# Turning the block mask on the matmul engine instead of by a DMA transpose

## The chip, the cores and the metric

The kernel runs on one core of one Trainium2 chip. The metric is the device time of one execution in microseconds. The engines are TensorE (PE, the matmul engine, with its weight loads shown apart as PEld), VectorE (DVE), ScalarE (ACT), GpSimd (POOL) and the sync engine (SP), which issues DMAs.

## The reference

One decoder block on x of 64 sequences of 128 tokens with 256 features, all fp32: gated causal cross attention with 16 heads against a context, then a gated feed-forward network of 1024 hidden units in 16 blocks, of which each token uses the four that a router picks.

```python
x = x + tanh(g_xattn) * attention(layernorm(x), ctx, ctx)      # 16 heads of 16, causal
xf = layernorm(x)
prob = softmax(xf @ w_router + b_router)
_, idx = top_k(prob, 4)
mask = (idx[:, :, None] == arange(16)).any(axis=1)             # token x block, 0 or 1
h = relu(einsum('nd,ebd->neb', xf, w1b) + b1b)                 # 16 blocks of 64
y = einsum('neb,ebd,ne->nd', h, w2b, mask) + b2
x = x + tanh(g_ffn) * y
```

## The kernel before

A tile is one sequence: 128 tokens on the 128 partitions. The kernel is one software pipeline over iterations i from -4 to 71. In iteration i each engine works, in an order written out by hand, on several tiles at once: scores of tile i + 1, exponentials of tile i, attention output of tile i - 1, the second layernorm of tile i - 2. The feed-forward part works on pairs of tiles (256 tokens): pair p has its hidden pieces 0 and 1 in iteration 2p + 5 and pieces 2 and 3 in iteration 2p + 6, and the output products of tile b stand in iteration b + 7. The engines are tied together by semaphores alone.

The matmul engine's order in an iteration is: scores (L273, L283), transposes of q (L240) and of k (L251), one hidden piece (L380 to L382; each product is split into three of high and low parts), half of an output tile (L401 to L403), in every second iteration the router's logits (L352), attention output (L313), shifted scores (L300), the transpose of the normalised x (L339), in every second iteration the turned logits (L360), the second hidden piece, the second output half, and the transposes of the attention output (L328). L313, L273 and L352 use narrow tiles of the array, the other large groups its full width.

Routing. In iteration 2p + 4 VectorE finds the four largest logits of each token of pair p (L611 to L623) and leaves them marked. ScalarE's choice (L485) turns the marks into a bf16 mask `used`, tokens on partitions, 128 columns for each of the pair's two tiles. The hidden units lie on partitions, so the mask must be turned. In iteration 2p + 5 the sync engine does so with one DMA transpose per pair into `used_all` (L793, in `used_spread`). It waits for the choice and, from pair 2 on, until the masks of two pairs before are done with. VectorE multiplies the hidden pieces by `used_all` in `hidden_masked` (L603), which waits for the transpose at a pair's first piece. The same sync queue then carries the maxima rows (`max_row`, L774: qT to qT, needed by the shifted scores), the loads and the stores.

A hidden piece is written to a bank that the engine may only reuse when L603 has read it (L374). ScalarE makes the relu parts h_high and hid (L475, L476) from the masked piece, and GpSimd makes h_low (L705). Bank M1 (number 7) is shared in turn by the transposes of q, the router's logits, the turned logits and the transposes of the attention output; M0 (number 6) by those of k, the attention output and the transposes of x. After iteration 64 hidden pieces and output tiles alternate between two banks each, since the scores' banks are free by then.

Of the kernel before, what the change touches and what calls it, by code (L numbers as in the profile page):

```python
# [33 lines left out]
def build(nc, A_x, A_ctx, A_g_xattn, A_g_ffn, A_w_router, A_b_router, A_w1T, A_b1, A_w2T, A_b2, out):  # L34
# [24 lines left out]
    with ctx:  # L59
# [92 lines left out]
        q_copied, k_copied, exp_done = sem("q_copied"), sem("k_copied"), sem("exp_done")  # L152
        att_copied, x_copied, xT_high_made = sem("att_copied"), sem("x_copied"), sem("xT_high_made")
        hid_clipped, w_high_made = sem("hid_clipped"), sem("w_high_made")
        route_copied, used_made, tanh_done = (sem(n) for n in ("route_copied", "used_made", "tanh_done"))

        numbers_set, filler_set = sem("numbers_set"), sem("filler_set")
        q_zeroed, q_levels_set, place_zeroed, mask_made = (sem(n) for n in (
# [70 lines left out]
        def _(pe):  # L229
# [87 lines left out]

            def out_transposed(b):
                s = b % 2
                pr = router_pair(b + 1)  # L320
                pe.wait_ge(att_copied, b + 1)
                pe.wait_ge(q_copied, min(b + 4, N + MAX_LAG))
                if pr is not None:
                    pe.wait_ge(clipped_made, PAIR * (pr + 1))
                if b + 3 >= N + MAX_LAG:
                    pe.wait_ge(att_made, b)
                for g in range(U):
                    turned = pe.transpose(banks[M1][:, g * P:(g + 1) * P], oT[:, s, g * S:(g + 1) * S], ident[:])  # L328
                turned.then_inc(att_turned, 1)
# [26 lines left out]
            def logits_transposed(p):  # L356
                if p == 0:
                    pe.wait_ge(adding_made, 1)
                pe.wait_ge(route_copied, p + 1)
                pe.matmul(out=banks[M1][:, 0:PAIR * PAD], lhsT=logitT[:], rhs=adding[:].rearrange("p t e -> p (t e)"),  # L360
                          start=True, stop=True).then_inc(route_turned, 1)

            def hidden(p, m):
                ps = p % 2
# [43 lines left out]
            for i in ITERATIONS:  # L408
                pr, pu = router_pair(i), used_pair(i)
                p, m = hidden_pair(i)  # L410
                out_b = out_tile(i)
                if i + 1 == 0:
                    pe.wait_ge(mask_made, 2 * U)
                if 0 <= i + 1 < N:
                    scores(i + 1)
                if 0 <= i + 2 < N + MAX_LAG:
                    q_transposed(i + 2)
                if 0 <= i + 2 < N:
                    k_transposed(i + 2)
                if p is not None:  # L420
                    hidden(p, m)
                if out_b is not None:
                    ffn_out(out_b, 0)
                if pr is not None:
                    router_logits(pr, i)
                if 0 <= i - 1 < N:
                    attention_out(i - 1)
                if 0 <= i < N:
                    shifted_scores(i)
                if 0 <= i - 2 < N:  # L430
                    x_transposed(i - 2)
                if pr is not None:
                    logits_transposed(pr)
                if p is not None:
                    hidden(p, m + 1)
                if out_b is not None:
                    ffn_out(out_b, 1)
                if 0 <= i - 1 < N:
                    out_transposed(i - 1)

        @block.scalar
        def _(act):
            def q_evacuated(b):
                act.wait_ge(q_turned, b + 1)
                act.copy(qT[:, b % TS, :], banks[M1][:]).then_inc(q_copied, 1)

            def k_evacuated(b):
                act.wait_ge(k_turned, b + 1)
                act.copy(kT[:, b % TS, :], banks[M0][:]).then_inc(k_copied, 1)

            def exponentials(b):
                act.wait_ge(rescored, b + 1)
                for half in range(2):
                    act.activation(weights[:, b % 2, half * 2 * HB:(half + 1) * 2 * HB, :].rearrange("p h q -> p (h q)"),  # L454
                                   score_banks[:, 2 * half:2 * half + 2].rearrange("p u n -> p (u n)"),
                                   ACT.Exp, scale=SCALE).then_inc(exp_done, 1)

            def out_copied(b):
                act.wait_ge(attended, b + 1)
                act.copy(oT[:, b % 2, :], banks[M0][:]).then_inc(att_copied, 1)  # L460

            def x_copies(b):
                p, t = divmod(b, PAIR)
                turned = banks[M0][:, 0:D].rearrange("p (c s) -> p c s", s=S)
                act.wait_ge(x_turned, b + 1)
                act.copy(xT[:, :, t, :], turned).then_inc(x_copied, 1)
                if t == 0 and p >= 2:
                    act.wait_ge(hidden_made, PIECES * (p - 1))
                act.copy(xT_high[:, p % 2, :, t, :], turned).then_inc(xT_high_made, 1)

            def hidden_parts(p, m):
                n = PIECES * p + m
                chunks = slice(PC * m, PC * (m + 1))
                act.wait_ge(hid_made, HC * p + PC * (m + 1))
                act.activation(h_high[:, p % 2, chunks], hid[:, n % 4], ACT.Relu)  # L475
                act.activation(hid[:, n % 4], hid[:, n % 4], ACT.Relu).then_inc(hid_clipped, 1)  # L476

            def choice(p):

                act.wait_ge(marked_made, PAIR * (p + 1))  # L480
                if p == 0:
                    act.wait_ge(numbers_set, 2)
                else:
                    act.wait_ge(used_turned, 16 * p)
                act.activation(used[:], marked[:].unsqueeze(3).to_broadcast([P, PAIR, BLOCKS, UNITS]), ACT.Relu,  # L485
                               scale=2.0 / TAKEN, bias=minus_one[:]).then_inc(used_made, 1)

            def weights_high(i):
                for n in pieces_of(i):
                    w, stage, high, _low = w_piece(n)  # L490
                    act.wait_ge(w_landed[w], 16 * W_LOADS[w])
                    act.copy(high, stage).then_inc(w_high_made, 1)

            act.wait_ge(x_landed[1], 16)
            act.dma_start(w1_stage[:].rearrange("p k e c r -> p k (e c r)"),
                          A_w1T.rearrange("(k p) n -> p k n", p=P)).then_inc(w_landed[0], 16)
            for i in ITERATIONS:
                pr, pu = router_pair(i), used_pair(i)
                p, m = hidden_pair(i)
                if 0 <= i + 2 < N + MAX_LAG:  # L500
                    q_evacuated(i + 2)
                if 0 <= i + 2 < N:
                    k_evacuated(i + 2)
                if pr is not None:
                    act.wait_ge(routed, pr + 1)
                    if pr == 0:
                        act.wait_ge(br_landed, 16 * PAIR)
                    act.activation(logitT[:], banks[M1][:, 0:S], ACT.Identity, bias=br_rows[:]).then_inc(route_copied, 1)
                if 0 <= i - 1 < N:
                    out_copied(i - 1)  # L510
                if 0 <= i < N:
                    exponentials(i)
                if p is not None:
                    hidden_parts(p, m)
                if pr is not None:
                    choice(pr)
                if 0 <= i - 2 < N:
                    x_copies(i - 2)
                if p is not None:
                    hidden_parts(p, m + 1)  # L520
                weights_high(i)
                if i == 0:
                    act.wait_ge(gates_landed, 32)
                    act.activation(tanh_g[:], gates[:], ACT.Tanh).then_inc(tanh_done, 1)

        @block.vector
        def _(dve):
# [63 lines left out]
            def hidden_masked(p, m):  # L591
# [3 lines left out]
                    dve.wait_ge(b1_landed, 16 * HC)  # L595
                    dve.wait_ge(w_low_made, 8)
                if m == 0:
                    dve.wait_ge(used_turned, 16 * (p + 1))
                if n >= 4:
                    dve.wait_ge(h_low_made, n - 3)  # L600
                for j in range(PC):
# [155 lines left out]
        def _(sync):  # L757
# [28 lines left out]
                sync.dma_start(br_rows[rows], A_b_router.rearrange("(e o) -> e o", o=1)).then_inc(br_landed, 16)  # L786
            for c in range(KC):
                sync.dma_start(w_router[:, c, 0:BLOCKS], A_w_router[c * P:(c + 1) * P, :]).then_inc(small_landed, 16)
            def used_spread(p):
                if p >= 2:  # L790
                    sync.wait_ge(hid_made, HC * (p - 1))
                sync.wait_ge(used_made, p + 1)
                sync.dma_start_transpose(used_all[:, p % 2].rearrange("p (t s) -> p t s", t=PAIR),  # L793
                                         used[:].rearrange("p t e r -> p (t e r)")).then_inc(used_turned, 16)

            for i in ITERATIONS:
                pu = used_pair(i)
                if pu is not None:
                    used_spread(pu)
                if 0 <= i < N:  # L800
                    max_row(i)
                if 0 <= i < HC // 4:
# [44 lines left out]
```

## Time and profile before

| | us |
|---|---|
| median of 3 runs | 750.77 |
| lowest and highest | 750.28, 751.03 |
| the profiled execution | 750.28 |
| its span in the trace | 748.6 |
| matmul engine busy | 717.0 |
| VectorE, ScalarE, GpSimd busy | 505.2, 430.8, 488.0 |
| chain that ended last, share of the matmul engine | 92% |

The span is what the trace covers of the profiled execution. Busy time counts an engine once even where its instructions overlap: matmuls are pipelined, so each lasts longer than the distance to the next, and it is that distance that adds up to the time of a stretch. The chain that ended last follows the last instruction back through whatever released each step.

### The profile page before, as it was taken

What the parts mean: (1) busy time and instruction counts of PE and PEld (TensorE: products, weight loads), DVE (VectorE), ACT (ScalarE), POOL (GpSimd) and SP (SyncE); (2) the same over time, 40 slices, a digit from 0 to 9 for tenths busy, and PEclk for the clock granted to TensorE, in tenths of its full rate; (3) what the DMA queues carried; (4) which work ended last, traced back from release to release, by engine and by line L of the source; (5) the groups of instructions that cost most, each with busy time, mean ns of one, the idle gap of its engine ahead of it and who ended that gap; (6) DMA issues with size and microseconds to landing.
All of it is one profiled execution on the core that took longest, in us unless ns stands there. A gap on an engine that the chain in (4) does not pass through costs nothing.

```text
span 748.6 us, 31053 instructions
## 1 busy us (share of the span) xinstructions
PE 717.0 (96%) x13512; PEld 668.4 (89%) x13512; DVE 505.2 (67%) x1428; ACT 430.8 (58%) x780; POOL 488.0 (65%) x663
## 2 busy tenths in 40 slices
PE   5669999999999999999999999999999999999888
PEld 4458999999999999999999999999999999999787
DVE  5468776776776676677677677667667767766552
ACT  3466566556556556656655655655665565565542
POOL 6587676676676667667667667666766766765542
PEclk9899999999999999999999999999999999999999
DMA  4312101111111111110111111011111011000010
GB/s 149 89 33 62 35 21 49 49 50 35 46 38 32 48 50 35 46 49 21 48 49 49 35 46 41 29 48 49 35 45 49 21 49 49 21 7 18 19 33 32
DMA packets 41397, 32.02 MB, mean 43 GB/s; under 512 B 15280, under 2 KB 41008, under 8 KB 41264
## 3 DMA queue, kind: packets, MB, share of 16 engines
q1 hardware_dynamic: 40992, 29.00, 13.0%
q8 instruction: 107, 1.75, 1.0%
q10 hardware_dynamic: 272, 1.05, 0.4%
q14 instruction: 26, 0.21, 0.1%
HBM read 19.03 MB, written 8.39 MB: 37 GB/s over the span
## 4 chain that ended last, share of the span: by engine, by line
PE 92%; ACT 3%; DMA 2%; DVE 1%; issue 1%; SPq 1%; POOLq 0%; POOL 0%; ACTq 0%
PE score_banks L300 10%; PE score_banks L273 9%; PE bank L380 8%; PE bank L401 8%; PE bank L403 8%; PE bank L402 8%; PE bank L382 8%; PE bank L381 7%; PE bank L313 7%; PE bank L240 5%; PE bank L328 3%; PE bank L251 3%; PE bank L339 3%; DMA qT<-qT 2%; PE score_banks L283 1%; ACT weights L454 1%
## 5 line engine op out<-in xcount | busy, mean ns | idle before, releaser
L698 POOL TENSOR_SCALAR_AFFINE_SELECT weights<-weights 128x1024 f32<-128x1024 f32 x128 | 138.0, 1103 | 150.2 <-ACT weights L454 150.2
L705 POOL TENSOR_TENSOR h_low<-hid,h_high 128x512 fp32r<-128x512 f32 x128 | 166.3, 1299 | 39.0 <-ACT hid L476 34.6
L603 DVE SCALAR_TENSOR_TENSOR hid<-bank,b_cols,used_all 128x256 f32<-128x256 f32 x248 | 108.1, 478 | 86.5 <-PE bank L382 84.3
L380 PE MATMUL bank<-xT_high,w_high 128*128 128x256 f32 x496 | 149.7, 302 | 0.0
L454 ACT ACTIVATE weights<-score_banks 128x1024 f32<-128x1024 f32 x128 | 124.3, 1023 | 38.9 <-PE score_banks L300 38.9
L401 PE MATMUL bank<-w_high,h_high 128*128 128x256 f32 x488 | 137.4, 281 | 3.2 <-DVE y_out L588 2.6
L382 PE MATMUL bank<-xT_high,w_low 128*128 128x256 f32 x496 | 139.4, 281 | 0.0
L381 PE MATMUL bank<-xT_low,w_high 128*128 128x256 f32 x496 | 139.0, 280 | 0.0
L403 PE MATMUL bank<-w_high,h_low 128*128 128x256 f32 x488 | 138.2, 283 | 0.0
L402 PE MATMUL bank<-w_low,h_high 128*128 128x256 f32 x488 | 137.9, 283 | 0.0
L460 ACT COPY oT<-bank 128x512 f32<-128x512 f32 x64 | 37.5, 586 | 115.1 <-PE bank L313 115.1
L401 PEld LDWEIGHTS bank<-w_high,h_high 128*128 128x128 f32 x488 | 92.2, 189 | 3.8 <-DVE y_out L588 3.0
L381 PEld LDWEIGHTS bank<-xT_low,w_high 128*128 128x128 f32 x496 | 94.0, 190 | 0.0
L380 PEld LDWEIGHTS bank<-xT_high,w_high 128*128 128x128 f32 x496 | 93.6, 189 | 0.1
L382 PEld LDWEIGHTS bank<-xT_high,w_low 128*128 128x128 f32 x496 | 93.2, 188 | 0.0
L403 PEld LDWEIGHTS bank<-w_high,h_low 128*128 128x128 f32 x488 | 92.0, 189 | 0.0
L402 PEld LDWEIGHTS bank<-w_low,h_high 128*128 128x128 f32 x488 | 91.8, 188 | 0.0
L475 ACT ACTIVATE h_high<-hid 128x512 fp32r<-128x512 f32 x128 | 82.7, 646 | 12.9 <-DVE hid L603 12.8
L548 DVE TENSOR_REDUCE q_pad<-score_banks 128x8 f32<-128x1024 f32 x64 | 77.8, 1216 | 10.9 <-PE score_banks L283 10.9
L686 POOL TENSOR_TENSOR rstd<-ve,half_power 128x1 f32<-128x1 f32 x128 | 77.5, 606 | 10.7
L476 ACT ACTIVATE hid<-hid 128x512 f32<-128x512 f32 x128 | 81.6, 638 | 0.0
L273 PEld LDWEIGHTS score_banks<-kT,qT 32*64 32x64 f32 x4096 | 63.5, 135 | 19.4 <-issue 17.2
(89 smaller groups left out, 1387.1 us busy)
## 6 DMA issues: line engine op xcount, KB each, us to landing
c_in<-in_ctx SPq DMA_DIRECT2D x32, 256.0 KB, 2.8
x_in<-in_x SPq DMA_DIRECT2D x32, 256.0 KB, 3.1
out_y<-y_out SPq DMA_DIRECT2D x31, 256.0 KB, 2.2
qT<-qT SPq DMA_DIRECT2D x128, 4.0 KB
w_stage<-in_w1T ACTq DMA_DIRECT2D x1, 1024.0 KB, 5.8
hid<-in_w2T SPq DMA_DIRECT2D x8, 128.0 KB, 2.7
used_all<-used SPq DMA_TRANSPOSE x32, 2.4
out_y<-y_out SPq DMA_DIRECT2D x2, 128.0 KB, 1.7
```

Of the source, the lines that this page charges most:

```text
L273: pe.matmul(out=score_banks[place_of, u, start:start + (1 + late) * HALF], lhsT=qT[rows, s, first + late * HALF:first + (1 + late) * HALF] ...
L380: pe.matmul(out=bank, lhsT=w1_high[:, k, c], rhs=high, start=k == 0, stop=False)
L381: pe.matmul(out=bank, lhsT=w1_high[:, k, c], rhs=low, start=False, stop=False)
L382: made = pe.matmul(out=bank, lhsT=w1_low[:, k, c], rhs=high, start=False, stop=k == KC - 1)
L401: pe.matmul(out=bank[:, 0:D], lhsT=high, rhs=w2_high[:, c, :], start=a, stop=False)
L402: pe.matmul(out=bank[:, 0:D], lhsT=high, rhs=w2_low[:, c, :], start=False, stop=False)
L403: made = pe.matmul(out=bank[:, 0:D], lhsT=low, rhs=w2_high[:, c, :], start=False, stop=z)
L454: act.activation(weights[:, b % 2, half * 2 * HB:(half + 1) * 2 * HB, :].rearrange("p h q -> p (h q)"), score_banks[:, 2 * half:2 * half + ...
L475: act.activation(h_high[:, p % 2, chunks], hid[:, n % 4], ACT.Relu)
L603: dve.scalar_tensor_tensor(hid[:, n % 4, j], hid_bank(n)[:, j * TOKS:(j + 1) * TOKS], b1_cols[:, c:c + 1], used_all[:, p % 2], ALU.add, AL ...
L698: pool.affine_select(out=w, in_=w, compare_op=ALU.is_ge, fill=0.0, base=0, pattern=[[0, 2 * HB], [1, S]], channel_multiplier=-1).then_inc( ...
L705: pool.tensor_tensor(h_low[:, p % 2, chunks], hid[:, n % 4], h_high[:, p % 2, chunks].bitcast(F32), ALU.subtract).then_inc(h_low_made, 1)
```

## The change

The mask is turned by two transposes of 128x128 bf16 per pair on the matmul engine (`used_transposed`, between the first output half and the attention output in iteration 2p + 5), into bank M1 read as bf16. ScalarE copies the result from there to `used_all`, behind the copies of q and k. VectorE's `hidden_masked` waits for this copy, and so do the transposes of the attention output, which reuse the bank. The sync engine's `used_spread` is gone. On ScalarE the choice moves from ahead of the x copies to the end of the iteration's work, behind the second hidden piece, and loses its wait for the transpose of the pair before.

```diff
             def out_transposed(b):
                 s = b % 2
-                pr = router_pair(b + 1)
+                pr, pu = router_pair(b + 1), used_pair(b + 1)
...
+                if pu is not None:
+                    pe.wait_ge(used_copied, pu + 1)
...
+            def used_transposed(p, i):
+                bank = banks[M1][:].bitcast(BF16)
+                pe.wait_ge(used_made, p + 1)
+                pe.wait_ge(q_copied, min(i + 3, N + MAX_LAG))
+                if i + 3 > N + MAX_LAG:
+                    pe.wait_ge(att_made, min(i - 1, N))
+                for t in range(PAIR):
+                    turned = pe.transpose(bank[:, t * S:(t + 1) * S],
+                                          used[:, t].rearrange("p e r -> p (e r)"), ident16[:])
+                turned.then_inc(used_turned, 1)
...
                 if out_b is not None:
                     ffn_out(out_b, 0)
+                if pu is not None:
+                    used_transposed(pu, i)
...
-                else:
-                    act.wait_ge(used_turned, 16 * p)
...
+                if pu is not None:
+                    act.wait_ge(used_turned, pu + 1)
+                    act.copy(used_all[:, pu % 2], banks[M1][:].bitcast(BF16)[:, 0:TOKS]).then_inc(used_copied, 1)
...
-                if pr is not None:
-                    choice(pr)
                 if 0 <= i - 2 < N:
                     x_copies(i - 2)
                 if p is not None:
                     hidden_parts(p, m + 1)
+                if pr is not None:
+                    choice(pr)
...
-                    dve.wait_ge(used_turned, 16 * (p + 1))
+                    dve.wait_ge(used_copied, p + 1)
...
-            def used_spread(p):
-                if p >= 2:
-                    sync.wait_ge(hid_made, HC * (p - 1))
-                sync.wait_ge(used_made, p + 1)
-                sync.dma_start_transpose(used_all[:, p % 2].rearrange("p (t s) -> p t s", t=PAIR),
-                                         used[:].rearrange("p t e r -> p (t e r)")).then_inc(used_turned, 16)
-
             for i in ITERATIONS:
-                pu = used_pair(i)
-                if pu is not None:
-                    used_spread(pu)
```

On the matmul engine, behind the first output half of iteration 7 (pair 1), before; a row names line, operation, output and inputs:

```order
231 L402 MATMUL bank<-w_low,h_high 128x256
232 L403 MATMUL bank<-w_high,h_low 128x256
233 L313 MATMUL bank<-weights,v_pad 32x128 [waits weighted,k_copied]
234 L313 MATMUL bank<-weights,v_pad 32x128 x7
235 L313 MATMUL bank<-weights,v_pad 32x128 [waits weighted]
236 L313 MATMUL bank<-weights,v_pad 32x128 x7
237 L300 MATMUL score_banks<-qT,kT 128x128 [waits max_found,max_landed1]
```

And now, at the same place (the lines of the changed kernel are some 13 higher from there on, so L416 is the old L403 and L372 is new):

```order
233 L415 MATMUL bank<-w_low,h_high 128x256
234 L416 MATMUL bank<-w_high,h_low 128x256
235 L372 MATMUL bank<-ident,used 128x128 [waits q_copied,used_made]
236 L372 MATMUL bank<-ident,used 128x128
237 L313 MATMUL bank<-weights,v_pad 32x128 [waits weighted,k_copied]
238 L313 MATMUL bank<-weights,v_pad 32x128 x7
239 L313 MATMUL bank<-weights,v_pad 32x128 [waits weighted]
240 L313 MATMUL bank<-weights,v_pad 32x128 x7
241 L300 MATMUL score_banks<-qT,kT 128x128 [waits max_found,max_landed1]
```

The two transposes of the mask stand between the last full-width product and the attention output, with their waits on the first.

On ScalarE, from the first relus of an even iteration to the exponentials of the next, before:

```order
109 L475 ACTIVATE h_high<-hid 128x512 [waits hid_made]
110 L476 ACTIVATE hid<-hid 128x512
111 L485 ACTIVATE used<-marked,minus_one 128x256 [waits used_turned,marked_made]
112 L466 COPY xT<-bank 128x2x128 [waits x_turned]
113 L469 CAST xT_high<-bank 128x2x128 [waits hidden_made]
114 L475 ACTIVATE h_high<-hid 128x512 [waits hid_made]
115 L476 ACTIVATE hid<-hid 128x512
116 L445 COPY qT<-bank 128x512 [waits q_turned]
117 L449 COPY kT<-bank 128x512 [waits k_turned]
118 L460 COPY oT<-bank 128x512 [waits attended]
119 L454 ACTIVATE weights<-score_banks 128x1024 [waits rescored]
```

And now:

```order
112 L490 ACTIVATE h_high<-hid 128x512 [waits hid_made]
113 L491 ACTIVATE hid<-hid 128x512
114 L481 COPY xT<-bank 128x2x128 [waits x_turned]
115 L484 CAST xT_high<-bank 128x2x128 [waits hidden_made]
116 L490 ACTIVATE h_high<-hid 128x512 [waits hid_made]
117 L491 ACTIVATE hid<-hid 128x512
118 L498 ACTIVATE used<-marked,minus_one 128x256 [waits marked_made]
119 L460 COPY qT<-bank 128x512 [waits q_turned]
120 L464 COPY kT<-bank 128x512 [waits k_turned]
121 L519 COPY used_all<-bank 128x256 [waits used_turned]
122 L475 COPY oT<-bank 128x512 [waits attended]
123 L469 ACTIVATE weights<-score_banks 128x1024 [waits rescored]
```

The choice stands four instructions later, at the end of the even iteration, and the copy of the turned mask stands ahead of the copy of oT in the next.

## Rows read from the trace of the kernel before

**Rows 1.** The page's part 1: engine, busy us, share of the span, instructions.

```profile
PE 717.0 (96%) x13512; PEld 668.4 (89%) x13512; DVE 505.2 (67%) x1428; ACT 430.8 (58%) x780; POOL 488.0 (65%) x663
```

**Rows 2.** Busy us of each engine from 100 to 700 us, then clock and DMA.

```profile
100.00:700.00 600.00, 599.10 (x11391) 561.32 (x11390) 415.74 (x1184) 357.01 (x648) 396.19 (x533) 1.00 0.13 40
```

**Rows 3.** Waits of the matmul engine from 75 us on: total us, times, longest.

```profile
PE bank L401 <- DVE y_out L588: 2.6, 2, 1.6
...
PE bank L360 <- ACT logitT L508: 0.5, 1, 0.5
```

**Rows 4.** Timeline of the matmul engine, two iterations: start us, us, instruction, count.

```profile
388.71 0.28 PE L403 MATMUL bank<-w_high,h_low 128*128 128x256 f32 x1
388.93 1.08 PE L313 MATMUL bank<-weights,v_pad 128*32 128x128 f32 x32
389.94 1.17 PE L300 MATMUL score_banks<-qT,kT 32*128 32x128 f32 x32
...
391.24 0.36 PE L380 MATMUL bank<-xT_high,w_high 128*128 128x256 f32 x1
...
399.54 0.29 PE L403 MATMUL bank<-w_high,h_low 128*128 128x256 f32 x1
...
400.00 1.06 PE L313 MATMUL bank<-weights,v_pad 128*32 128x128 f32 x32
400.98 1.17 PE L300 MATMUL score_banks<-qT,kT 32*128 32x128 f32 x32
```

**Rows 5.** The DMA transposes on the page, in the queue's timeline and its waits.

```profile
used_all<-used SPq DMA_TRANSPOSE x32, 2.4
...
383.57 1.19 SPq L793 DMA_TRANSPOSE used_all<-used  x1
...
SPq L774 <- ACT qT L445: 331.7, 64, 9.3
```

**Rows 6.** Timeline of VectorE in the steady part and the tail; idle before in brackets.

```profile
388.94 0.88 DVE L603 SCALAR_TENSOR_TENSOR hid<-bank,b_cols,used_all 128x256 f32<-128x256 f32 x2
...
392.94 0.88 DVE L603 SCALAR_TENSOR_TENSOR hid<-bank,b_cols,used_all 128x256 f32<-128x256 f32 x2 [2.46 <-PE bank L382]
...
730.46 0.88 DVE L603 SCALAR_TENSOR_TENSOR hid<-bank,b_cols,used_all 128x256 f32<-128x256 f32 x2 [2.12 <-DMA used_all<-used]
```

**Rows 7.** Matmul engine: all L328 (min, median, max ns), then transposes and neighbours.

```profile
L328 PE MATMUL bank<-ident,oT x256: 270/273/329, 30.7 to 712.8; 128*128 128x128 f32 x128
...
383.35 0.60 PE L328 MATMUL bank<-ident,oT 128*128 128x128 f32 x4
383.88 0.99 PE L273 MATMUL score_banks<-kT,qT 32*64 32x128 f32 x51
...
712.48 0.60 PE L328 MATMUL bank<-ident,oT 128*128 128x128 f32 x4
712.83 0.36 PE L380 MATMUL bank<-xT_high,w_high 128*128 128x256 f32 x1
...
717.46 0.28 PE L403 MATMUL bank<-w_high,h_low 128*128 128x256 f32 x1
717.58 0.38 PE L339 MATMUL bank<-ident,xn 128*128 128x128 f32 x2
717.72 0.36 PE L380 MATMUL score_banks<-xT_high,w_high 128*128 128x256 f32 x1
...
733.35 0.28 PE L380 MATMUL bank<-xT_high,w_high 128*128 128x256 f32 x1
```

**Rows 8.** Timeline of ScalarE: an x copy, and the idle time before oT.

```profile
383.39 0.37 ACT L466 COPY xT<-bank 128x256 f32<-128x256 f32 x1
...
390.07 0.59 ACT L460 COPY oT<-bank 128x512 f32<-128x512 f32 x1 [3.25 <-PE bank L313]
```

**Rows 9.** Waits for the maxima rows' landing: the whole run, and the last one.

```profile
PE score_banks L300 <- DMA qT<-qT: 5.1, 6, 2.3
...
70.64 1.17 PE L300 MATMUL score_banks<-qT,kT 32*128 32x128 f32 x32 [0.20 <-DMA qT<-qT]
```

More of the change, by code:

```diff
@@ L154, in build @@
         hid_clipped, w_high_made = sem("hid_clipped"), sem("w_high_made")
-        route_copied, used_made, tanh_done = (sem(n) for n in ("route_copied", "used_made", "tanh_done"))
+        route_copied, used_made, used_copied, tanh_done = (sem(n) for n in ("route_copied", "used_made", "used_copied", "tanh_done"))
         numbers_set, filler_set = sem("numbers_set"), sem("filler_set")
```

## The prediction

> **What bounds the kernel now.** I read three views, in this order. First the page: the matmul engine is busy for 717.0 of 748.6 us, 96 per cent [rows 1]. That is an average, so the second view is the stretch from 100 to 700 us, the steady part. There the matmul engine is busy 599.10 of 600.00 us at a granted clock of 1.00, while VectorE has 184 us, ScalarE 243 us and GpSimd 204 us to spare [rows 2]. Third, the list of what the matmul engine waited for from 75 us on: five entries between 2.6 and 0.5 us, 5.5 us together, and all of them behind 690 us, where the last tiles drain [rows 3]. The reader should see that between 75 and 690 us no other engine, no DMA and no semaphore sets the pace. The pace is the sum of the distances from one matmul to the next: 400.98 - 389.94 = 11.04 us for an iteration [rows 4], some 22.1 us for the two in which the routing step runs once.
>
> Two consequences. Taking work or waits from another engine or a queue gives nothing in those 615 us. And what is added to the matmul engine's own stream is paid in full.
>
> **What the change removes.** 32 DMA transposes, each with 1.19 us of issue on the sync queue and 2.4 us to land [rows 5]. Who was held by them? Readers: the wait list has one wait on their landing, 2.1 us of VectorE before the mask at 730.46 us, in the tail [rows 6]. The result of that mask is next needed when its bank is used again, by L380 at 733.35 [rows 7], 2.0 us after the mask's end, so the end of the kernel did not pay it. In the steady part the transfer starts at 383.57 and has landed by about 386.0, 2.9 us before its reader at 388.94 [rows 5, 6]. The sync queue: the maxima row (L774) comes behind the transpose on it. All 64 maxima rows waited for the qT copy on ScalarE [rows 5], which they could not have done had the transpose held them beyond it. The matmul engine, through shared memory ports: all 256 transposes of L328, half of which run beside or just before such a transfer, lie between 270 and 329 ns with a median of 273 [rows 7]; a slowed half would stand out. The removal is worth 0.
>
> **What it adds on the matmul engine.** 64 transposes of 128x128 bf16, two per pair, between the last L403 of the first FFN half and L313 (weights times values). No row shows a bf16 transpose, so I price two from their neighbours.
>
> Before, L403 to L313 takes 388.93 - 388.71 = 0.22 us [rows 4]. L403 takes 0.12 between its like (717.58 - 717.46 [rows 7]); the other 0.10 is the change to narrow tiles.
>
> Lower row: in the tail two fp32 transposes of the same size (L339) stand between full-width matmuls, at 717.58, and L380 follows at 717.72: two cost 0.14 us [rows 7]. A transpose lasts 273 ns, but they overlap, and only the distance of the starts is paid. Half the bytes may make them a little quicker: 0.12, my estimate from this row.
>
> Upper rows: (a) in the other iteration the router's matmuls stand at exactly this place. L403 to L313 is then 400.00 - 399.54 = 0.46 instead of 0.22, so 0.24 more; L313 itself then takes 0.98 instead of 1.01, so 0.21 net [rows 4]. (b) The change to narrow tiles may hide less behind a transpose than behind a 256-column matmul. Four L328 before it take 383.88 - 383.35 = 0.53; four before full-width L380 take 712.83 - 712.48 = 0.35 [rows 7]. So the change costs 0.18 behind transposes against 0.10 behind L403, which adds 0.08 to the 0.14: 0.22. High end 0.27: the 0.24 and 0.03, the size by which L313 differs between the two iterations.
>
> I take 0.20 us per pair: near the two upper rows, since these transposes do stand before such a tile change, and a little below them, since the operands are half as wide. The first pair, at about 61 us, stands where the matmul engine next waits for the maxima row to land (the ramp, where it did so in six places [rows 9]); I count it as free. The other 31 pay: 31 x 0.20 = 6.2 us. Ends: 31 x 0.12 = 3.7 and 31 x 0.27 = 8.4.
>
> A rule to weigh. The trace's row gives 273 ns for one transpose [rows 7]. The Trainium skill, "TensorE: Matmul & The Clock Gate", Part 4, has about 275 ns for a 128x128 bf16 transpose in a kernel's context, and says that transposes don't count as activity for the clock. As a duration the trace agrees. Taken as the price in the stream it would make the sum 62 x 0.275 = 17 us by that page in place of 6.2.
>
> **What it adds and moves elsewhere, costed at nothing.** ScalarE gets 32 copies of 128x256 out of PSUM; the nearest row is L466 at 0.37 us. The copy falls at about 389.2 us, and ScalarE sits idle for 3.25 us before 390.07 [rows 8]: hidden. Behind it on ScalarE stands the copy of oT, which waits for L313 and so becomes due later than it. The choice (L485) moves behind two copies and two relus, from 383 to about 385; ScalarE's work up to there is the same in sum, and the matmul engine asks for the result only at 388.83: over 3 us to spare. The x copies and the last relus come earlier by the choice's half microsecond, for which nobody waits. The new wait on L328 for the copy is met 4 us before L328 runs.
>
> VectorE's mask of the pair's first hidden piece (L603, 388.94) is where a new wait stands in the chain. It waits for the transposes (last start about 388.90, and 0.27 for the duration: 389.2) and the copy (389.6), so it starts about 0.7 later and ends at 390.5. Queued behind it on VectorE are the q normalisation and x_parts, which end near 391.2; VectorE is then idle, before for 2.46 us until 392.94 [rows 6], which absorbs the 0.7. The matmul engine needs the mask when the next hidden piece reuses the bank, at 391.24 before [rows 4] and 391.44 now. 0.9 us to spare: hidden. Were this cover gone, each pair would pay the excess. In the tail the last mask moves from 730.46 to about 731.3 (the transposes now stand behind the FFN half that ends at 730.5) and ends at 732.2, against the need at 733.35 plus 0.2 [rows 6, 7].
>
> **Sum.** The profiled execution took 750.28 us, its span 748.6; the 1.7 us around it stay. 750.28 + 6.2 = 756.5. The median of the three runs lies 0.49 above that execution, so on the median I give 757.0; with the ends, 754.5 and 759.2.
>
> **Rivals.**
> 1. Faster: the DMA transposes disturb more than is seen. The place would be the ramp, where the matmul engine waits 5.1 us in six places for the maxima row, which shares a queue with them, and VectorE's 2.1 us in the tail [rows 6, 9]. If both went entirely and two transposes cost 0.14: 750.8 - 7.2 + 4.3 = 747.9. It decides for faster from 0.18 us a pair down, with all of 7.2 regained. Against: of the six waits only the one of 0.20 at 70.64 stands behind the first transfer [rows 9]. Chance 0.02.
> 2. No change: the transposes slip into gaps, under 0.05 us a pair: 751 to 752. Against: 0.90 us without a matmul in 600 [rows 2], and L339's 0.14. Chance 0.03.
> 3. A new wait on the matmul engine: transposes, copy and mask outlast the 0.9 us. With 0.3 over it, 31 x 0.3 = 9 us on top: 766. For it speaks that three engines now hand over in a row in each pair, with no more than 0.05 us counted for a handover; against, the spare time. Chance 0.04.
> 4. The transposes cost their duration and not their distance, which is the page's figure above taken as a price: 62 x 0.273 = 17 us, 768. Against: L339's two in 0.14. Chance 0.03. For the clock there is no sign: granted 1.00, with 14 transposes in every iteration already.
> The forecast, slower by 3.7 to 8.4 us, has 0.88.
>
> **How the numbers follow.** About 0.2% (1.5 us) is what a measurement of this kernel can tell from no change. Slower: 0.88 + 0.04 + 0.03 = 0.95; same 0.03; faster 0.02. The range holds the forecast's ends and some half microsecond around them, 754.0 to 760.0; the rivals, 0.12 in all, stay outside.
>
> **What would show it.** In the steady part two iterations take about 22.3 us in place of 22.1, and L403 to L313 behind a pair's first hidden pieces about 0.42 in place of 0.22. Each new transpose lasts near 0.27 but steps under 0.1. The matmul engine still waits for nothing from 75 to 690 us; a wait of L380 there for VectorE's mask would be rival 3. The mask starts 0.6 to 0.8 us later, behind ScalarE's new copy. The ramp's waits for qT stay near 5 us. The prediction is wrong if a bf16 transpose before a change of tiles costs something else than its fp32 neighbours.

## The result and the profile after

| | before | changed |
|---|---|---|
| median, us | 750.9 (4 runs) | 762.46 (4 runs, 758.12 to 763.47) |
| ratio, 95% interval | | 1.0139 (1.0096 to 1.0183) |
| profiled execution, its span | 750.28, 748.6 | 759.15, 757.4 |
| matmul engine busy | 717.0 | 726.0 |
| VectorE busy | 505.2 | 532.1 |

The changed kernel is slower, as forecast, but by some 11 us and not 6 (11.6 by the medians, 10.4 by the ratio); the time lies outside the range of 754.0 to 760.0. A repetition beside another set of runs (below) gave 1.0113 (1.009 to 1.0136). From here on a loss in us is the ratio's excess times the median of the kernel before in the same set of runs. The part of the page that answers to [rows 1], with VectorE's surprising 27 us more from the same 1428 instructions, and the steady stretch that answers to [rows 2]:

```profile
PE 726.0 (96%) x13576; PEld 675.0 (89%) x13576; DVE 532.1 (70%) x1428; ACT 442.0 (58%) x812; POOL 488.3 (64%) x663
```

```profile
100.00:700.00 600.00, 599.78 (x11350) 560.75 (x11349) 438.29 (x1177) 363.58 (x670) 393.48 (x531) 1.00 0.12 36
```

The matmul engine is as full as before and at the same clock of 1.00, so the loss is again a longer stream. Its chain, at the shifted scores (L300) of five iterations of the changed kernel (start us, us, what):

```profile
360.45 1.10 PE score_banks L300 x32
371.76 1.10 PE score_banks L300 x32
382.79 1.10 PE score_banks L300 x32
394.09 1.10 PE score_banks L300 x32
405.14 1.10 PE score_banks L300 x32
```

Two iterations take 405.14 - 382.79 = 22.35 us. The chain of the kernel before has

```profile
378.95 1.10 PE score_banks L300 x32
390.01 1.10 PE score_banks L300 x32
401.05 1.10 PE score_banks L300 x32
```

which is 22.10. The 0.25 us over 31 pairs make 7.7 of the 8.8 us by which the spans differ. All of the 0.25 lies in the iteration that holds the transposes (11.30 to 11.31 in place of 11.06), in two places. The first is the one looked for. Timeline of the matmul engine there, answering to [rows 4]:

```profile
392.67 0.28 PE L416 MATMUL bank<-w_high,h_low 128*128 128x256 f32 x1
392.79 0.29 PE L372 MATMUL bank<-ident,used 128*128 128x128 bf16 x2
393.01 1.08 PE L313 MATMUL bank<-weights,v_pad 128*32 128x128 f32 x32
```

L416 (the old L403) to L313 takes 0.34 in place of 0.22: two transposes cost 0.12 us. The second place stands ahead of them, at the start of the output half (L414 is the old L401):

```profile
391.13 0.28 PE L395 MATMUL bank<-xT_high,w_low 128*128 128x256 f32 x1
391.27 0.19 PEld L414 LDWEIGHTS bank<-w_high,h_high 128*128 128x128 f32 x1
391.27 0.39 PE L414 MATMUL bank<-w_high,h_high 128*128 128x256 f32 x1
391.49 0.28 PE L415 MATMUL bank<-w_low,h_high 128*128 128x256 f32 x1
```

The same place before:

```profile
387.30 0.28 PE L382 MATMUL bank<-xT_high,w_low 128*128 128x256 f32 x1
387.30 0.19 PEld L401 LDWEIGHTS bank<-w_high,h_high 128*128 128x128 f32 x1
387.41 0.28 PE L401 MATMUL bank<-w_high,h_high 128*128 128x256 f32 x1
```

L414 lasts 0.39 us and L415 follows 0.22 later. Before, L401 lasted 0.28 and L402 followed after 0.12. The stream is broken there: 391.49 - 391.13 = 0.36 where it was 387.53 - 387.30 = 0.23, so 0.13 us more. The weight load (PEld) shows what is late: before, it started with the previous matmul, 0.11 ahead of its own; now it starts 0.14 behind the previous matmul, at 391.27, and its own matmul starts with it. L414, its weight load included, waits for VectorE's y_out (L604, the old L588). VectorE's timeline says why, in the same iteration, with GpSimd's beside it:

```profile
388.58 1.58 DVE L581 SCALAR_TENSOR_TENSOR x<-att,tanh_g,x_in 128x256 f32<-128x256 f32 x1
390.19 0.43 DVE L545 BATCH_NORM_STATS2 stats<-x 128x6 f32<-128x256 f32 x1
390.65 0.18 DVE L547 BATCH_NORM_AGGREGATE mv<-stats 128x2 f32<-128x6 f32 x1
390.75 0.47 DVE L604 SCALAR_TENSOR_TENSOR y_out<-bank,tanh_g,x_b 128x256 f32<-128x256 f32 x1
```

```profile
387.17 1.28 POOL L721 TENSOR_TENSOR h_low<-hid,h_high 128x512 fp32r<-128x512 f32 x1
388.60 1.27 POOL L721 TENSOR_TENSOR h_low<-hid,h_high 128x512 fp32r<-128x512 f32 x1
```

L581 (the old L565, x2 = att * gate + x) lasts 1.58 us. GpSimd's second h_low starts 0.02 after it and ends at 389.87; L581 ends 0.29 after that. So y_out ends at 390.75 + 0.47 = 391.22, which is 0.09 past the moment (391.13) at which the weight load of L414 would have started. Before, the same pair of instructions ran so:

```profile
384.73 0.49 DVE L565 SCALAR_TENSOR_TENSOR x<-att,tanh_g,x_in 128x256 f32<-128x256 f32 x1
```

```profile
385.16 1.28 POOL L705 TENSOR_TENSOR h_low<-hid,h_high 128x512 fp32r<-128x512 f32 x1 [0.55 <-ACT hid L476]
```

There h_low came 0.43 us later, when x2 was nearly done. GpSimd waited for ScalarE's relu (L476), and that relu stood behind the choice, which the change moves away. Almost nothing of this is in the list of waits: x2 is counted as busy, and the matmul engine's short gap is covered by the modelled ends of its matmuls. The list from 75 us on has one hint; the two rows of the timeline under it show where it comes from:

```profile
PE bank L414 <- DVE y_out L604: 3.3, 4, 1.6
...
547.48 0.48 DVE L604 SCALAR_TENSOR_TENSOR y_out<-bank,tanh_g,x_b 128x256 f32<-128x256 f32 x1 [0.25 <-issue]
...
548.01 0.39 PE L414 MATMUL bank<-w_high,h_high 128*128 128x256 f32 x1 [0.22 <-DVE y_out L604]
```

These are four waits where [rows 3] has two; the new ones are the 0.22 at 548.01 and one of 0.54 at 703.98. At 547.48 VectorE's y_out is once 0.25 late for no visible reason. The kernel before has such a delay of y_out once too, and there the matmul engine did not wait. So the collision leaves no room for a chance delay, and that is part of the 1.1 us which the 7.7 leave open.

What shows the collision itself is the count by line (answers of both kernels, x2's line):

```profile
L565 DVE SCALAR_TENSOR_TENSOR x<-att,tanh_g,x_in x64: 484/485/1483, 32.1 to 713.9; 128x256 f32<-128x256 f32 x64
```

```profile
L581 DVE SCALAR_TENSOR_TENSOR x<-att,tanh_g,x_in x64: 484/1010/1585, 32.3 to 722.4; 128x256 f32<-128x256 f32 x64
```

From 98 us on every second x2 of the changed kernel lasts 1.57 or 1.58 and every other 0.48: 28 x 1.1 = 30.8 us. VectorE's extra busy time is 26.9, since the line of xn (old L573, new L589) saves 3.8. The matmul engine's trace has the same count: from 98 to 704 us 28 matmuls of L414 last over 0.35 us, one behind each blocked x2, and none of L401 did before. So the collision's part is paid 28 times and not 31, and 31 x 0.12 + 28 x 0.13 = 7.4 is nearer than 7.7. The rule is in the Trainium skill, "SBUF — State Buffer", section "SBUF: two separate sides": a VectorE instruction with two SBUF inputs and a GpSimd instruction that reads SBUF exclude each other; the one that starts first holds the port pair for the whole instruction, and the other is blocked. The trace agrees on who can collide: x2 has att and x_in in SBUF and is blocked; y_out, whose first input is in PSUM, took 0.46 at 385.82 in the kernel before, in the middle of an h_low. It does not agree on who starts first: by the record x2 did, by 0.02 us each time; but the profile's spans on GpSimd are rough.

### The profile page after: what moved, and what is told of

The parts are those of the page before. It is cut to its first block, busy times and chain, and to the rows that moved or that the text cites. A ratio compares the mean times of both kernels' runs of the same rounds, so it can differ in the third digit from the quotient of the medians.

```text
span 757.4 us, 31152 instructions
## 1 busy us (share of the span) xinstructions
PE 726.0 (96%) x13576; PEld 675.0 (89%) x13576; DVE 532.1 (70%) x1428; ACT 442.0 (58%) x812; POOL 488.3 (64%) x663
## 3 DMA queue, kind: packets, MB, share of 16 engines
q1 hardware_dynamic: 31776, 26.90, 11.6%
## 4 chain that ended last, share of the span: by engine, by line
PE 92%; ACT 3%; DVE 2%; DMA 1%; issue 1%; SPq 0%; POOLq 0%; POOL 0%; ACTq 0%
PE score_banks L300 10%; PE score_banks L273 8%; PE bank L414 8%; PE bank L313 8%; PE bank L393 8%; PE bank L416 8%; PE bank L415 8%; PE bank L395 7%; PE bank L394 7%; PE bank L240 5%; PE bank L251 4%; PE bank L330 3%; PE bank L341 3%; ACT weights L469 1%; PE score_banks L283 1%; PE bank L354 1%
## 5 line engine op out<-in xcount | busy, mean ns | idle before, releaser
L414 PE MATMUL bank<-w_high,h_high 128*128 128x256 f32 x488 | 140.6, 288 | 4.0 <-DVE y_out L604 3.3
L395 PE MATMUL bank<-xT_high,w_low 128*128 128x256 f32 x496 | 139.4, 281 | 0.0
L416 PE MATMUL bank<-w_high,h_low 128*128 128x256 f32 x488 | 137.9, 283 | 0.0
L415 PE MATMUL bank<-w_low,h_high 128*128 128x256 f32 x488 | 137.8, 282 | 0.0
L414 PEld LDWEIGHTS bank<-w_high,h_high 128*128 128x128 f32 x488 | 92.2, 189 | 6.6 <-DVE y_out L604 4.1
L395 PEld LDWEIGHTS bank<-xT_high,w_low 128*128 128x128 f32 x496 | 93.4, 188 | 0.0
L416 PEld LDWEIGHTS bank<-w_high,h_low 128*128 128x128 f32 x488 | 92.1, 189 | 0.0
L415 PEld LDWEIGHTS bank<-w_low,h_high 128*128 128x128 f32 x488 | 91.9, 188 | 0.0
L700 POOL TENSOR_SCALAR ve<-mv 128x1 f32<-128x1 f32 x128 | 28.6, 224 | 88.5 <-DVE mv L547 88.4
L273 PEld LDWEIGHTS score_banks<-kT,qT 32*64 32x64 f32 x4096 | 63.0, 134 | 19.3 <-issue 17.1
```

The lines of the kernel that those rows point to most:

```text
L273: pe.matmul(out=score_banks[place_of, u, start:start + (1 + late) * HALF], lhsT=qT[rows, s, first + late * HALF:first + (1 + late) * HALF] ...
L395: made = pe.matmul(out=bank, lhsT=w1_low[:, k, c], rhs=high, start=False, stop=k == KC - 1)
L414: pe.matmul(out=bank[:, 0:D], lhsT=high, rhs=w2_high[:, c, :], start=a, stop=False)
L415: pe.matmul(out=bank[:, 0:D], lhsT=high, rhs=w2_low[:, c, :], start=False, stop=False)
L416: made = pe.matmul(out=bank[:, 0:D], lhsT=low, rhs=w2_high[:, c, :], start=False, stop=z)
```

## The experiments

Theory A: the loss has two parts, 0.12 to 0.13 us for the transposes and as much for the collision of x2 with h_low, which comes from moving the choice. Theory B: it is all the cost of the transposes and the copy behind them.

### The choice put back

```diff
+                if pr is not None:
+                    choice(pr)
                 if 0 <= i - 2 < N:
                     x_copies(i - 2)
                 if p is not None:
                     hidden_parts(p, m + 1)
-                if pr is not None:
-                    choice(pr)
```

> The changed kernel with the choice put back ahead of the x copies on ScalarE; nothing else differs. Theory A (half of the loss is a collision): the choice's move lets the second relu of an even iteration end 0.5 us earlier, so GpSimd starts h_low together with VectorE's x2 operation, which then lasts 1.58 in place of 0.48 us and holds up y_out and with it the matmul engine. With the choice back, x2 lasts 0.48 again in all iterations, and two iterations take 22.10 + 0.12 = 22.22 us: 750.9 + 31 x 0.12 = 754.6, and the runs lie as close together as those of the kernel before. Theory B (the loss is the transposes themselves and the copy that follows them): no gain, 762 as the changed kernel.

Measured: 755.95 us against 752.37 of the kernel before in the same set of runs, 1.005 (1.0031 to 1.0068), so 3.8 us. x2 and the chain:

```profile
L581 DVE SCALAR_TENSOR_TENSOR x<-att,tanh_g,x_in x64: 483/485/1471, 33.6 to 719.5; 128x256 f32<-128x256 f32 x64
```

```profile
371.52 1.10 PE score_banks L300 x32
382.57 1.10 PE score_banks L300 x32
393.76 1.10 PE score_banks L300 x32
```

The collision is gone, h_low starts at 388.78 behind x2's 388.36, and two iterations take 393.76 - 371.52 = 22.24 us. That is the price of the transposes alone: 0.14 a pair, 31 x 0.14 = 4.3. Other pairs of this trace take 22.21 to 22.25, most of them 22.23, so a reading of one pair is good to some 0.01 or 0.02. The expected narrow spread did not show (753.47 to 756.79), but the kernel before spread as much beside it (748.76 to 754.63).

### The choice moved in the kernel before

The reverse edit in the kernel with the DMA transposes.

> The kernel before with only the choice moved to the end of the iteration; the DMA transposes stay. Theory A: the collision alone; x2 lasts 1.58 us in every second iteration, the first product of the output half behind it starts 0.12 us late, two iterations take 22.22 us in place of 22.10: about 754.6, with runs spread as those of the changed kernel. Theory B: the move costs nothing, 751.

Measured: 756.4, 1.0065 (1.0043 to 1.0088), 4.9 us. x2 has a median of 996 ns, with 1.58 at 386.42 beside h_low at 386.44, and two iterations take 391.82 - 369.60 = 22.22:

```profile
369.60 1.10 PE score_banks L300 x32
380.63 1.10 PE score_banks L300 x32
391.82 1.10 PE score_banks L300 x32
```

The move of one 0.51 us instruction on an engine that is idle for 40 per cent of the time costs about as much as the transposes, without any transpose on the matmul engine. Theory B falls.

### The path over y_out

```diff
-                if 0 <= i - 2 < N:
-                    attention_added(i - 2)
                 if 0 <= i - OUT_LAG - 1 < N:
                     finished(i - OUT_LAG - 1)
+                if 0 <= i - 2 < N:
+                    attention_added(i - 2)
```

> The changed kernel with the output tile's last step on VectorE (y_out) put ahead of the attention output's steps, so that it no longer stands behind x2. Theory A, with the path over y_out: x2 still lasts 1.58 us in every second iteration, but the matmul engine no longer pays: two iterations 22.22 us, 754.6 in all. If the collision is paid over another path (the maxima or the norm behind x2), it stays near 760. Theory B: 762.

Measured: 755.11, 1.0037 (1.0017 to 1.0056), 2.8 us. The collision is still there, and the matmul engine no longer pays for it, with 392.14 - 369.90 = 22.24:

```profile
L581 DVE SCALAR_TENSOR_TENSOR x<-att,tanh_g,x_in x64: 484/1013/1585, 32.3 to 716.6; 128x256 f32<-128x256 f32 x64
```

```profile
369.90 1.10 PE score_banks L300 x32
380.95 1.10 PE score_banks L300 x32
392.14 1.10 PE score_banks L300 x32
```

Here y_out ends at 386.03, long before L414 at 389.42. What is left, 0.14, is the price of the transposes alone, so x2's delay reaches the matmul engine over y_out and the bank that it frees, and over nothing else that these readings can tell from 0.

### GpSimd's operation in halves

```diff
-                pool.tensor_tensor(h_low[:, p % 2, chunks], hid[:, n % 4], h_high[:, p % 2, chunks].bitcast(F32),
-                                   ALU.subtract).then_inc(h_low_made, 1)
+                for j in range(PC):
+                    c = PC * m + j
+                    made = pool.tensor_tensor(h_low[:, p % 2, c], hid[:, n % 4, j], h_high[:, p % 2, c].bitcast(F32),
+                                              ALU.subtract)
+                made.then_inc(h_low_made, 1)
```

> The changed kernel with each h_low of GpSimd (128x512) as two operations of 128x256. Theory A says VectorE's x2 is blocked until the GpSimd operation that got the memory port first has ended. With halves it is blocked for some 0.65 us and not 1.1: x2 lasts about 1.1 us, y_out comes 0.45 earlier, and the matmul engine does not wait: about 755. If x2 is slowed in proportion to shared work rather than blocked by one operation, it stays at 1.58 (the second half follows at once) and the time at 762.

Measured: 756.93, 1.0079 (1.0049 to 1.0109), 5.9 us by four runs; the profiled execution took 755.26 and its two iterations 392.92 - 370.69 = 22.23. In the iteration of the collision:

```profile
387.52 1.03 DVE L581 SCALAR_TENSOR_TENSOR x<-att,tanh_g,x_in 128x256 f32<-128x256 f32 x1
```

```profile
387.55 0.73 POOL L723 TENSOR_TENSOR h_low<-hid,h_high 128x256 fp32r<-128x256 f32 x1
```

1.03 in place of 1.58, though the second half follows the first at once (at 388.23): x2 ends at 388.55, 0.27 after the first half's end, as it ended 0.29 after the whole h_low in the changed kernel. So it is let in at the end of the one operation that it collided with. It is blocked by an operation, and not slowed by a share. y_out now ends at 389.61 and the weight load of L414 starts at 390.09, so nothing waits. The price moves too: in other iterations x2 now lasts about 0.53, and GpSimd is busy 26 us longer.

### The changed kernel once more

> The changed kernel itself once more, beside the same runs of the kernel before as the three below. If its loss is the sum of the two parts seen apart (0.13 us for two transposes, 0.12 us for the collision, both 30 to 31 times), it lies some 7.7 us above the kernel before. If the two together cost more than apart, as 762.46 against 750.9 would have it, it lies 10 us or more above.

Measured: 759.08 against 750.72, 1.0113 (1.009 to 1.0136), 8.5 us, beside 7.4 to 7.7 by the two parts in the traces and 3.8 + 4.9 = 8.7 by the runs of the parts alone. The first comparison, 11.6 us by its medians, had four runs on each side; its interval, 7.2 to 13.7, contains the parts' sum. Why three of those runs were above 761 is not shown by the trace, which is of an execution of 759.15, and stays open.

### Without the transfers

The kernel before without L793 and its waits; the mask is set to ones once (the routing is computed but not used).

> The kernel before without the DMA transposes and the waits for them: VectorE multiplies by a mask of ones set once, so the routing is computed and not used. My step that the removal is worth 0: no change in time, and two iterations take 22.10 us. Rival (the transfers disturb another engine or a queue): faster by 1.5 us or more.

Measured: 750.31 against 750.72, 1.0003 (0.9989 to 1.0017). Two iterations take 391.32 - 369.22 = 22.10:

```profile
369.22 1.10 PE score_banks L300 x32
391.32 1.10 PE score_banks L300 x32
```

The removal of the DMA transposes is worth nothing, to within 1.3 us.

### Four transposes

In this run and the next the choice is put back as well, so both compare with the first experiment (22.24 us for two iterations).

```diff
-                for t in range(PAIR):
+                for t in [*range(PAIR)] * 2:
                     turned = pe.transpose(bank[:, t * S:(t + 1) * S],
```

> The changed kernel with the choice ahead, and each pair's two transposes done twice over into the same place. If a transpose costs the distance of starts, 0.06 to 0.07 us each, two iterations take 22.23 + 0.13 = 22.36 us and the whole 4 us more than with two. If most of the 0.13 is a fixed cost of breaking the stream for them, two more cost under 0.05 a pair, 1.5 us in all. If they cost their duration (0.27 each), 17 us more.

Measured: 758.27, 1.01 (1.0081 to 1.0119), 7.5 us, 3.7 more than with two by the ratios of two sets of runs. The chain gives 373.24 - 350.91 = 22.33, 0.09 over the 22.24 with two. The timelines with four, and with two:

```profile
371.70 0.28 PE L416 MATMUL bank<-w_high,h_low 128*128 128x256 f32 x1
371.83 0.40 PE L372 MATMUL bank<-ident,used 128*128 128x128 bf16 x4
372.15 1.08 PE L313 MATMUL bank<-weights,v_pad 128*32 128x128 f32 x32
```

```profile
370.11 0.28 PE L416 MATMUL bank<-w_high,h_low 128*128 128x256 f32 x1
370.23 0.29 PE L372 MATMUL bank<-ident,used 128*128 128x128 bf16 x2
370.44 1.08 PE L313 MATMUL bank<-weights,v_pad 128*32 128x128 f32 x32
```

372.15 - 371.70 = 0.45 against 370.44 - 370.11 = 0.33 is 0.12 for two more; the chain says 0.09. One bf16 transpose costs 0.05 to 0.06 us in the stream, though the whole group of two lasts 0.29. The same rows price the change to narrow tiles behind the transposes. From the first transpose to L313 the four take 372.15 - 371.83 = 0.32 and the two 370.44 - 370.23 = 0.21, so two steps are 0.11 and the change is 0.21 - 0.11 = 0.10, as much as behind L403 before. By these rows there is no fixed price of having the group there; by the chain it is at most 0.02 to 0.05, near what a reading of one pair can tell.

### Between full-width products

```diff
+                if pu is not None:
+                    used_transposed(pu, i)
                 if out_b is not None:
                     ffn_out(out_b, 0)
-                if pu is not None:
-                    used_transposed(pu, i)
```

> The changed kernel with the choice ahead, and the two transposes moved ahead of the output half, so that full-width products stand on both sides and no change of tile width follows them. If the change to narrow tiles hides less behind a transpose (my 0.08 a pair), two iterations take about 22.16 us, 2 us less in all. If not, 22.23 as with the transposes ahead of the narrow tiles. VectorE's mask then starts as early as before the change.

Measured: 755.64, 1.0071 (1.0055 to 1.0087), 5.3 us; two iterations 393.93 - 371.66 = 22.27. The place that I held to be cheaper is no cheaper, rather 0.03 dearer. The cost is there, but it sits behind the first product that follows:

```profile
368.77 0.28 PE L395 MATMUL bank<-xT_high,w_low 128*128 128x256 f32 x1
368.89 0.29 PE L372 MATMUL bank<-ident,used 128*128 128x128 bf16 x2
368.98 0.37 PE L414 MATMUL bank<-w_high,h_high 128*128 128x256 f32 x1
369.18 0.28 PE L415 MATMUL bank<-w_low,h_high 128*128 128x256 f32 x1
```

L414 starts 0.09 after the two transposes but L415 only 0.20 after L414, where 0.12 is the usual step. 369.18 - 368.77 = 0.41 against 0.23 is 0.18 a pair. As in the collision, the weight load of L414 has lost its lead: it starts at 368.96, 0.02 ahead of its matmul in place of 0.11.

### A version without the change

The order of VectorE's steps from the third experiment, in the kernel before. It is the control of that experiment too: if the new order gained something by itself, the 22.24 there would prove less.

> The kernel before with VectorE's last step of an output tile (y_out) put ahead of the attention output's steps; DMA transposes and the early choice stay. In the steady part nothing waited for y_out, so two iterations stay at 22.10 us. Of the drain's 2.6 us of waits for y_out a part should go: 0 to 2 us less than the kernel before, at most 0.3%. If it is slower, the x2 chain behind it (the norm, the maxima) had less room than I think.

Measured: 751.34 against 751.15, 0.9996 (0.9981 to 1.0011). Two iterations take 404.11 - 382.01 = 22.10 us, as before. No gain; no version here beats the kernel before.

## Why the prediction was wrong

**The bound, and the removal at 0: right.** The matmul engine's stream sets the pace, the removal of the DMA transposes is worth nothing (without the transfers, 1.0003), and neither the ramp's waits for qT's landing (4.3 us in place of 5.1) nor the copy on ScalarE holds up the matmul engine in the steady part.

**The price of two transposes, 0.20 us: too high.** They cost 0.14 by the chain and 0.12 by the timeline, near the lower end. 31 pairs make 4.3 us and not 6.2 (measured alone, 3.8). Both upper rows misled. The router's insertion holds eight narrow fp32 matmuls. They start at 399.75, 0.21 behind L403 as L313 did, so the 0.24 is their own. The extra 0.08 for the change of tiles behind a transpose does not exist here: with four and with two transposes the change comes to 0.10, as behind L403. It was read from L328 to L273, another pair of groups, where the 0.18 goes along with 0.17 us that the view puts down to issue before the weight loads of L273. And between full-width products the price was higher, not lower.

**The step that failed: "The x copies and the last relus come earlier by the choice's half microsecond, for which nobody waits".** I asked who waits for the moved instruction and not what the instructions behind it trigger when they come sooner. GpSimd's h_low follows the last relu at once. It came 0.4 us earlier against x2 (0.02 behind its start in place of 0.43), and blocked it for 1.1 us. y_out stands behind x2 on VectorE. I had not priced its room: before, it ended at 385.82 + 0.46 = 386.28 and the weight load of L401 started at 387.30, so 1.02 us, a little less than the block. What was put at nothing costs 0.12 to 0.13 us in each of 28 pairs, 3.6 us in all (measured alone, 4.9). The rows were at hand: L565 at 384.73 and h_low at 385.16 with 0.55 us of idle time before it for the relu, and a maximum of 1483 ns on x2's line beside a median of 485. The chance of a new wait on the matmul engine went to the mask (rival 3), and the mask held: it started at 393.74 in place of about 393.0 and nobody waited.

**The range.** It covered the unknown of one term and no cost on the queues past which the choice was moved. Two errors of opposite sign, 2 us too much for the transposes and some 4 us missed, bring the forecast of 757.0 to 759. The repetition measured 759.08, inside the range, and that would have been luck: the sum was near and one of its two parts was not in it. The 762.46 of the first comparison lies 3 us above what the parts explain, and these 3 us stay open.

## What to carry to other kernels

Where one engine's stream is the bound and all others have a third of the time to spare, an instruction that comes earlier can still cost: follow what it releases, on which engine and beside which other operation that will run. VectorE operations with two inputs in SBUF, and GpSimd operations that read SBUF, should be checked against each other in time whenever either moves; the minimum, median and maximum of a line show whether it already collides somewhere. And the slack of every bank that the bound engine reuses belongs in the working, not only that of the bank that the change touches.

## What the runs showed of the hardware

A blocked instruction is counted as busy: VectorE's busy time rose by 27 us with no instruction added. The one that starts first in the trace need not be the one that gets in: x2 at 388.58 was blocked by an h_low at 388.60 (starts on GpSimd are recorded roughly). With 0.43 us of lead, at 384.73 in the kernel before, x2 was not blocked. A 128x128 bf16 transpose steps 0.05 to 0.06 us in a running stream, against 0.07 for fp32 [rows 7]. In a full stream the weight load of a matmul starts 0.11 us ahead of it, and a wait for a bank holds up that load too: y_out was only 0.09 us too late for it, and the matmul's start looks only some 0.02 late (0.14 behind L395 in place of 0.11), but its successor came another 0.10 late, 0.13 in all. The room before such a wait is to be counted to the weight load's start and not to the matmul's.
